# All six weight remainders of a routed expert on VectorE, none on GpSimd, in a float32 recurrence and mixture-of-experts kernel

## The reference

```python
xn = _layernorm(x, axis=-1)
s = _L0_attn_ref(xn, W1, b1, W2, b2, init_h)          # recurrence, hidden size 1024
# experts
shared_out = _swiglu(x, shared_gate_w, shared_up_w, shared_down_w)
topk_ids = jnp.argmax(x @ gate_w, axis=-1)            # one of 32 experts
xs = x * sigmoid(max logit)
order = jnp.argsort(topk_ids); sorted_x = xs[order]
g = _grouped_mm(sorted_x, routed_gate_w, tokens_per_expert)   # 512 -> 1024
u = _grouped_mm(sorted_x, routed_up_w, tokens_per_expert)     # 512 -> 1024
d = _grouped_mm(silu(g) * u, routed_down_w, tokens_per_expert)  # 1024 -> 512
out = x + s * silu(shared_out + d[inv])
```

## Time and profile before

| what | value |
|---|---|
| median of 3 runs | 4409.26 us (4401.57 to 4411.47) |
| span of the profiled execution, first to last instruction | 4402.1 us |
| routed sweep in the span, first matmul of tile 0 to the end | 2791.4 to 4402.1 us |
| PE busy, whole span | 4061.1 us (92%) |
| DVE busy, whole span | 2581.3 us (59%) |
| ACT busy, whole span | 1813.5 us (41%) |
| POOL busy, whole span | 1453.2 us (33%) |

### The profile page before, as it was taken

How to read it: one execution, slowest core, us unless ns; L and a number is a source line. 1 busy time by engine, 2 the same in 40 slices (tenths; PEclk the granted TensorE clock), 3 DMA queues, 4 the chain that set the end, 5 groups by cost and what they waited for, 6 DMA issues and landing times. The chain is left out here.

```text
span 4402.1 us, 56358 instructions
## 1 busy us (share of the span) xinstructions
PE 4061.1 (92%) x17851; PEld 3246.7 (74%) x17852; DVE 2581.3 (59%) x3328; ACT 1813.5 (41%) x2581; POOL 1453.2 (33%) x1245
## 2 busy tenths in 40 slices
PE   7999999999788999999999999699999999999997
PEld 6888888888666777777777777577777777777776
DVE  4323232322488888888888888555556565655564
ACT  3222222222255555555555555333334333433432
POOL 2010110101055222222222222444445455554553
PEclk9999999999899999999999999899999999999999
DMA  4121211211120100000110000545455455555552
GB/s 162 60 86 67 76 71 71 83 60 77 48 61 25 40 29 29 29 29 29 39 48 29 29 29 10 217 174 183 172 181 198 165 199 203 201 204 183 181 200 86
DMA packets 197719, 447.12 MB, mean 102 GB/s; under 512 B 19705, under 2 KB 36281, under 8 KB 193794
## 3 DMA queue, kind: packets, MB, share of 16 engines
q1 hardware_dynamic: 165170, 346.24, 22.0%
q0 software_dynamic: 32464, 99.94, 6.3%
HBM read 345.38 MB, written 104.68 MB: 102 GB/s over the span
## 5 line engine op out<-in xcount | busy, mean ns | idle before, releaser
L85 PE MATMUL gate<-xT,w_hi 128*128 128x512 f32 x1536 | 601.3, 391 | 8.2 <-DVE w_lo L95 8.2
L86 PE MATMUL gate<-xT,w_hi 128*128 128x512 f32 x1536 | 600.1, 391 | 0.0
L87 PE MATMUL gate<-xT,w_lo 128*128 128x512 f32 x1536 | 599.6, 390 | 0.0
L1259 DVE TENSOR_TENSOR wlo<-raw,whi 128x2048 fp32r<-128x2048 f32 x128 | 488.2, 3814 | 23.0 <-ACT whi L1255 23.0
L521 DVE TENSOR_TENSOR h_act<-h_act,psU 128x512 f32<-128x512 f32 x128 | 88.0, 687 | 688.6 <-PE psU L87 688.5
L1466 PE MATMUL tY<-whi,thT 128*128 128x512 f32 x1264 | 431.9, 412 | 31.3 <-DVE thT L1399 27.4
L1255 ACT ACTIVATE whi<-raw 128x2048 fp32r<-128x2048 f32 x192 | 367.5, 1915 | 42.4 <-PE tU L87 22.3
L1100 PE MATMUL rpsY<-w_hi,rhT 128*128 128x512 f32 x512 | 222.5, 434 | 134.8 <-ACT rhT L899 134.8
L85 PEld LDWEIGHTS gate<-xT,w_hi 128*128 128x128 f32 x1536 | 290.0, 189 | 71.3 <-issue 5.8
L86 PEld LDWEIGHTS gate<-xT,w_hi 128*128 128x128 f32 x1536 | 289.9, 189 | 61.7
L87 PEld LDWEIGHTS gate<-xT,w_lo 128*128 128x128 f32 x1536 | 289.8, 189 | 61.6
(11 more groups left out here) (205 smaller groups left out, 9727.7 us busy)
## 6 DMA issues: line engine op xcount, KB each, us to landing
raw<-in_L_ffn_routed_gate_w SPq DMA_DIRECT2D x64, 1024.0 KB, 5.4
raw<-in_L_ffn_routed_up_w SPq DMA_DIRECT2D x64, 1024.0 KB, 5.0
raw<-in_L_ffn_routed_down_w SPq DMA_DIRECT2D x64, 1024.0 KB
xT_dram<-xT SPq DMA_DIRECT2D x16, 2048.0 KB, 6.3
xT<-xT_dram SPq DMA_DIRECT2D x14, 2048.0 KB, 7.8
x_in<-in_L_attn_x SPq DMA_DIRECT2D x16, 1024.0 KB, 6.0
xs_dram<-x_in SPq DMA_DIRECT2D x16, 1024.0 KB, 4.4
ss_dram<-y_sb SPq DMA_DIRECT2D x64, 256.0 KB, 2.0
```

The source lines that it names most:

```text
L85: pe.matmul(out, w[0], x[0], start=start, stop=False)
L86: pe.matmul(out, w[0], x[1], start=False, stop=False)
L87: return pe.matmul(out, w[1], x[0], start=False, stop=stop)
L1259: eng.tensor_tensor(wlo[q][:], raw[q][:], whi[q][:], ALU.subtract).then_inc(wlo_done[q], 1)
```

## The change

`BY_POOL` is removed. GpSimd's program loses its four places of `split_lo`. In VectorE's program the part U0 comes between `h_mul(1)` and G1, and D0 between `zb` and the product `yo`; in tile 0 the same for the first expert, U0 after `x_lo(0)`, and D0 ahead of D1. The line numbers shift: L1259 becomes L1258, L1395 becomes L1388, L1399 becomes L1392, L1375 becomes L1367, L1420, L1423 and L1426 become L1415, L1419 and L1422.

```diff
     G0, U0, G1, U1, D0, D1 = range(PARTS)
-    BY_POOL = (U0, D0)
...
             fetch(xg[:], xs_dram, at_next[:], xg_loaded)
-            split_lo(pool, U0, 0)
...
                 fetch(xr[:], x_rows, at_this[:], xr_loaded)
-                if isinstance(t, int):
-                    split_lo(pool, D0, 0)
-                if switch:
-                    split_lo(pool, U0, e + 1)
-                    split_lo(pool, D0, e + 1)
...
             def lo(q, e):
-                if q not in BY_POOL:
-                    split_lo(dve, q, e)
+                split_lo(dve, q, e)
...
             lo(G0, 0)
             x_lo(0)
+            lo(U0, 0)
             lo(G1, 0)
...
                 if isinstance(t, int):
+                    lo(D0, 0)
                     lo(D1, 0)
                 h_mul(1)
+                nxt(U0)
                 nxt(G1)
...
                 dve.tensor_tensor(zb[:], psY[:], ss[:, 0:D], ALU.add).then_inc(z_done, 1)
+                nxt(D0)
                 dve.wait_ge(zs_done, t + 1)
```

## The result

The changed kernel takes 4273.59 us (4270.95 to 4275.86, 4 runs) against 4406.34 us before in the same comparison, a ratio of 0.970, 95% interval 0.969 to 0.972. That is 133 us less, where 4295 us (4268 to 4320) was forecast. The direction and the mechanism are as forecast.

What follows compares the result with a forecast made beforehand. VectorE's order at each turnover of weights was taken as the bound. Savings of 93 us (31 pairs), 4 (tile 0) and 17 (half clock) sum to 114: span 4402.1 to 4288, median 4295 us, range 4268 to 4320.

Steps and rivals of the forecast that it cites:

- The mechanism: At weight turnovers: VectorE's subtraction waits until GpSimd's ends, then runs alone; without GpSimd's each takes 2.3 us.
- U0 ahead of G1, the switch tile: Switch tile: `h_lo(1)` starts at 16.63 instead of 17.44, so the tile takes 18.96 us, not 19.77.
- D0 between `zb` and `yo`, the next tile: Tile behind a switch: `th` starts at 26.83, not 29.80; 0.44 us of stall is left, the tile takes 18.31.
- Half clock: TensorE partly at 1.2 instead of 2.4 GHz behind the stall for `th`: 17 of 28 us outside the typical pair gained.
- Tile 0: First tile: PE's waits of 2.9 and 3.8 us for GpSimd's U0 and D0 shrink, saving 4 us.
- (1): VectorE's chain in a pair: five subtractions stay long for another reason, at 3.73 us each 4553 us; chance 0.04.
- (2): VectorE's extra work delays GpSimd's gather `ss`; only a landing of 13 us would cost, 68 us: 4363; chance 0.05.
- (3): Tiles behind a switch: remaining stalls are enough for the half clock, the 17 us are not gained: 4312; chance 0.17.
- (4): Switch pairs: PE's queue covers the 0.4 us and the branches, leaving no stall: 4236; chance 0.04.
- (5): PE's idle time moves to another wait of the same length, such as `zb` or the tile's-end branch; chance 0.03.

Runs made afterwards that it cites:

- `pool_reads`: Changed kernel plus, at GpSimd's two old places in a switch tile, an unneeded multiplication of a scratch tile by itself; 4399.17 us, ratio to before 0.9993.
- `pool_writes`: Changed kernel plus, at GpSimd's two old places, unneeded memsets of a scratch tile, four per switch tile; 4274.08 us.
- `u0_only`: Kernel before with only U0's subtraction moved to VectorE, D0's left on GpSimd; 4418.44 us, ratio to before 1.0028.
- `d0_late`: Changed kernel with D0's subtraction moved from between `zb` and the product `yo` to behind the sum `yo`, ahead of D1's; 4295.78 us.
- `d0_only`: Kernel before with only D0's subtraction moved to VectorE, U0's left on GpSimd; 4293.20 us, ratio to before 0.974.
- `u0_early`: Changed kernel with U0's subtraction moved from behind `h_mul(1)` to directly behind G0's; 4234.59 us, ratio to before 0.961.

## Why the prediction was right, and where it was off

**The mechanism** held. VectorE's long subtractions were waits for GpSimd's; without those, each of the 192 takes 2.28 us, and `pool_reads` and `pool_writes` show it with VectorE's program unchanged. Three terms were sized too small, by 11, 4 and 2 us.

**U0 ahead of G1, the switch tile.** Forecast 18.96 us, measured 18.97.

**D0 between `zb` and `yo`, the next tile.** Forecast 18.31, measured 17.96. This is the term that was off by most: the prediction took 2.58 us from D1's start to `th`, which contains an idle time of 0.28 and a full 2.29. Measured are 2.20 (3356.99 - 3354.79). The idle time belonged to the kernel before, in which D1 itself had waited 0.30 us for ScalarE: the two come together in all 31 pairs there and in `u0_only`. The same working had D1 start without that wait, and so had to leave out the idle time too. D1 also starts 0.09 earlier than forecast (24.16 against 24.25). `th` starts at 26.36 and not 26.83, and with the 0.74 from there to PE's transposes that is 27.10, just ahead of the 27.13 at which PE is due, so that the stall of 0.44 us does not exist (measured 27.25, with no idle time before it). A pair saves 3.35 instead of 3.01 us, 104 instead of 93 us.

**Half clock.** Forecast 17 of the 28 us outside the typical pair. The 77 tiles' total fell by 124.8 us; less 104 for the pairs, 21 came from there. Before, 13 of the 31 tiles behind a switch had a granted clock of 0.86 to 0.93 and no other of the 77 tiles had one below 1.00; the drops in busy stretches of which the prediction speaks are not there. The time lost, (1 - clock) x length summed over these tiles, is 24 us. In the changed kernel none has, and no tile behind a switch takes more than 18.6 us, where before they went up to 24.5. The 7 us that are left outside the pairs are at the ends of the loops of eight tiles. The drops go with the stall for `th`: stalls of 2.1 to 3.6 us before, drops in 13 of 31 tiles; 2.8 to 3.1 in `u0_only`, in 22; 0.55 to 0.65 in `d0_late`, in none. `d0_only` has its two drops without such a stall, behind switch tiles of 20.98 us. No run changed the clock alone, so that the 21 us are the clock's by this account and not by a test.

**Tile 0.** Forecast 4 us. It took 26.03 us (2789.18 to 2815.21) instead of 31.95, 5.9 less. PE's waits for `wlo` fell from 6.7 us in all to 3.2. Most of the rest is busy time of PE, 22.5 us instead of 25.2, at a granted clock of 0.85 in this tile instead of 0.76. The clock of this one tile is 0.93 in `pool_writes`, which has the same program for PE and VectorE and takes 26.45 us, so that the 2.7 us can't be put down to the change. The sweep also began 2.2 us earlier in this execution, ahead of anything that the change touches.

The sum of what was measured: 104 + 21 + 6 + 2 = 133 us of the span (4402.1 to 4269.3), against 114 forecast. The medians of the runs are also 133 us apart. Of the 19 us between, 11 are the pairs, 4 the clock, 2 tile 0 and 2 the earlier start.

**The rivals.** (1), VectorE as the bound, is refuted: the mean of all subtractions is 2283 ns and the longest takes 2.29 us. (2), late gathers: `ss` is issued 5.9 us after the sum (3360.08 against 3354.18), 7.5 us ahead of the tile's end, where 5.2 + 2.2 and 6.3 were forecast; `zb` never waits for a DMA. (3), the half clock stays, did not occur: it is 1.00 in all 77 tiles. (4), no stall left, came true by half. The stall for `th` is gone. For `thT` 0.26 us of idle time stayed, and 0.41 at the start of the next tile; the switch tile takes 1.1 us more than a plain one, and in `u0_early` that is gone too. (5), no change, did not occur: no row of waits grew by such an amount.

## What to carry to other kernels

Work given from VectorE to GpSimd was no relief here, where VectorE's instruction has two inputs in SBUF and GpSimd's reads SBUF too: look whether the same instruction has two durations in the trace, and whether the long one ends a full short duration after GpSimd's. When two such instructions meet twice, taking away one meeting can lengthen the other, so judge the pair of tiles and not the tile. And once the chain is short, look at the order in VectorE's queue: moving one line brought 39 us more. Put the subtraction where that engine waits anyway, not right ahead of the operation that TensorE waits for.

## What the runs showed of the hardware

GpSimd's small instructions and DMA issues take longer beside VectorE's subtraction too. In the changed kernel:

```profile
3337.29 2.80 POOL L1263 DMA_INDIRECT shared_and_s<-ss_dram,at_this  x1 [0.83 <-POOL at_this L1295]
...
3343.41 2.59 POOL L1263 DMA_INDIRECT xg<-xs_dram,at_next  x1 [1.87 <-PE tX L1433]
3355.12 2.00 POOL L1270 COPY at_out<-scatter_at 128x1 int32 x1 [9.13 <-DVE yo L1422]
3358.04 1.02 POOL L1273 DMA_INDIRECT out<-yo,at_out  x1 [0.92 <-POOL at_out L1270]
```

The issue at 3337.29 ends at 3340.09, 0.87 after the subtraction that began at 3336.93 and took 2.29; the one at 3343.41 ends at 3346.00, 0.94 after the first of the two from 3342.86 ended (at 3345.06), as if it had slipped between the two. Without a subtraction beside it such an issue takes 0.97 to 1.00 us. A copy of one element per partition takes 2.00 us beside D1's subtraction and 0.18 without, in all 31 pairs. VectorE's subtractions beside these issues stay at 2.28 us. And a GpSimd multiplication of a 128x2048 float32 tile by itself takes 3.61 us, against 4.6 for the subtraction of two tiles; whether that is the operation or the single tile no run tells.
